# A convolution and expert kernel: the second product token-major, its rows returned by way of HBM, halo and store issues moved between the queues

## The reference

```python
x = x + conv3x3(gn(x), L0_weight) + L0_bias
x = x + conv3x3(gn(x), L1_weight) + L1_bias
h = gelu(einsum('bend,edf->benf', gn(x), w1) + b1)   # exact gelu; e = channel, n = image row, d = 256 columns
x = x + einsum('benf,efd->bend', h, w2) + b2         # f = 1024
x = x + conv3x3(gn(x), L3_weight) + L3_bias
```

## Time and profile before

| | |
|---|---|
| median of 3 runs | 577.23 us |
| the profiled execution's own time | 576.91 us |
| its span, first to last instruction | 575.1 us |
| TensorE busy | 520.0 us, 90% |
| VectorE, ScalarE, GpSimd busy | 374.1, 291.8, 159.1 us |
| steps 0 to 7 with the first transposes | 0 to 143 us |
| first expert, pair 0 | 143 to 178 us |
| experts to the end of the second part | 178 to 447 us |
| third and fourth part | 447 to 499 us |
| steps 8 to 11 and the stores | 499 to 575 us |

### The profile page before, as it was taken

The page is one execution under the profiler, slowest core; times in us unless marked ns, Lnnn a source line. Parts: engine busy times, 40 slices in busy tenths (PEclk is TensorE's granted clock), DMA queues, the critical chain, the costliest instruction groups (busy, mean ns, idle before and its releaser), DMA issues.

```text
span 575.1 us, 9042 instructions
## 1 busy us (share of the span) xinstructions
PE 520.0 (90%) x3326; PEld 255.5 (44%) x3326; DVE 374.1 (65%) x644; ACT 291.8 (51%) x354; POOL 159.1 (28%) x181
## 2 busy tenths in 40 slices
PE   0879999896979999999999999999999989978990
PEld 0534445364544444444444444444444545445440
DVE  4969999888766395194293392481547598678541
ACT  2599988333635453353362361461444828766510
POOL 4679888853270000000000000000000001677610
PEclk9889999898899999999999999999999999989996
DMA  8845555533020122022011112102123300134769
GB/s 327 324 111 146 150 132 139 143 101 147 0 75 1 73 74 74 0 73 73 0 73 73 31 42 73 73 0 73 74 74 108 112 0 2 45 81 107 242 200 349
DMA packets 14168, 57.41 MB, mean 100 GB/s; under 512 B 3116, under 2 KB 3244, under 8 KB 11052
## 3 DMA queue, kind: packets, MB, share of 16 engines
q1 hardware_dynamic: 11820, 49.30, 26.9%
q10 hardware_dynamic: 2316, 7.68, 3.7%
HBM read 30.03 MB, written 8.39 MB: 67 GB/s over the span
## 4 chain that ended last, share of the span: by engine, by line
PE 62%; DVE 19%; ACT 5%; POOL 4%; DMA 3%; issue 2%; ACTq 1%; SPq 1%; POOLq 0%; DVEq 0%
PE PS L1007 28%; PE PS L978 27%; DVE X L665 6%; DVE ST L626 6%; PE PS L878 2%; POOL XN L360 2%; ACT XN L439 2%; PE PS L952 2%; DMA X<-x 2%; PE PS L936 2%; PE PS L885 1%; DVE X L681 1%; ACT SCR L444 1%; DVE XT L674 1%; DVE SM L641 1%
## 5 line engine op out<-in xcount | busy, mean ns | idle before, releaser
L978 PE MATMUL PS<-XT,W1S 128*128 (+1 forms) x768 | 172.0, 383 | 1.7 <-DVE XT L674 1.7
L1007 PE MATMUL PS<-HID,W2S 128*128 128x512 f16 x768 | 170.8, 379 | 1.6 <-DVE W2S L688 1.6
L476 ACT ACTIVATE SCR<-PS,CONST 128x512 f32<-128x512 f32 x128 | 87.0, 686 | 64.4 <-PE PS L978 27.8
L978 PEld LDWEIGHTS PS<-XT,W1S 128*128 128x128 f16 x768 | 75.6, 99 | 91.1 <-issue 4.7
L1007 PEld LDWEIGHTS PS<-HID,W2S 128*128 128x128 f16 x768 | 75.1, 98 | 87.5 <-issue 1.8
L360 POOL TENSOR_TENSOR XN<-SCR,XN 128x1024 f16<-128x1024 f32 (+1 forms) x61 | 100.4, 1670 | 26.5 <-ACT SCR L444 26.5
L688 DVE SCALAR_TENSOR_TENSOR W2S<-W2F,W2S 128x2048 f16<-128x2048 f32 x10 | 22.9, 2291 | 114.6 <-ACT W2S L472 114.6
L333 POOL MEMSET HALO<- 48x520 f16 x12 | 6.3, 526 | 316.8 <-PE PS L978 316.3
L626 DVE BATCH_NORM_STATS2 ST<-X 128x6 f32<-128x512 f32 x128 | 81.5, 681 | 9.4 <-DMA X<-x 8.2
L439 ACT ACTIVATE XN<-X,SC 128x1024 f16<-128x1024 f32 (+1 forms) x61 | 64.1, 1050 | 33.9 <-POOL SC L351 27.6
L665 DVE SCALAR_TENSOR_TENSOR X<-PS,X 128x512 f32<-128x512 f32 x96 | 59.7, 680 | 21.5 <-PE PS L900 21.5
(11 more groups left out here) (47 smaller groups left out, 442.9 us busy)
## 6 DMA issues: line engine op xcount, KB each, us to landing
W1F<-w SPq DMA_DIRECT2D x10, 1024.0 KB, 4.7
W2F<-w SPq DMA_DIRECT2D x10, 1024.0 KB, 4.8
HALO<-XN SPq DMA_DIRECT2D x48, 129.9 KB
out<-X ACTq DMA_DIRECT2D x12, 512.0 KB, 6.8
HALO<-XN SPq DMA_DIRECT2D x48, 121.8 KB
X<-x SPq DMA_DIRECT2D x2, 2048.0 KB, 19.0
HALO<-XN SPq DMA_DIRECT2D x42, 64.9 KB
HALO<-XN SPq DMA_DIRECT2D x42, 60.9 KB
```

The costliest lines, as they stand in the source:

```text
L476: act.activation(SCR[:, ft % 2, 0:CH], bank(ft % G_RING), ACT.Gelu, bias=BT[:, ds(e * FT + ft, 1)], scale=1.0 / (XS * WS)).then_inc(gelu_o ...
L978: mm = pe.matmul(bank(ft % G_RING), W1S[:, w, h * NF + ft * P:h * NF + (ft + 1) * P], rhs, start=(n == 0), stop=(n == 3 * DH - 1))
L1007: mm = pe.matmul(bank(G2_BANK + h), W2S[:, w, ft * NW + h * P:ft * NW + (h + 1) * P], HID[slot][:, part, ft], start=(ft == 0 and part == 0 ...
```

## The change

- **Second product.** `output` now takes 128 tokens of HID as weights and the 256 features of W2S as the moving operand: for each pair 4 blocks k x 8 tiles x 3 products = 96 matmuls of 256 columns, in place of 48 of 512. A block's sum lies in bank 4 + k % 2, and ScalarE copies it out (`copy_out`, [128 tokens, 256]); 64 such copies stand for 32 of [128, 512].
- **The way back.** There are no result transposes. SyncE stores each block to a scratch tensor `yd` in HBM (64 DMAs of 128 KB, in rows of 512 bytes); an image is then read back into YX in four DMAs: the rows of experts 0 to 6 (two of 56 x 16 KB, issued by ScalarE) and the rows of expert 7 (two of 8 x 16 KB, issued by SyncE). VectorE adds YX to X (`add_outputs`, both inputs in SBUF) and takes the statistics. The bias b2 is added to X beforehand, one image in each of experts 1 to 4 (`add_bias`, 32 instructions of VectorE).
- **Halos and stores.** ScalarE now issues the thirds of the first half of every step 8 to 11, between its fourth and fifth piece (4 DMAs a step); SyncE issues the thirds of the second half, step 11's too. All stores are SyncE's: image 0 and the first half of image 1 before the halos of step 11, the rest behind them.
- **Order.** In step 7 VectorE splits W1 before the statistics of the first half; in the first expert W2's split comes earlier, ScalarE writes half of the high parts of HID, and pre-transposes are spread anew. Step 8 to 11 have 7 PSUM banks in turn, not 5.

The diff, cut to its core:

```diff
-G2_BANK, TR_BANK, STAT_BANK = 4, 6, 5
-L3_BANKS = (1, 2, 3, 0, 4)
+G2_BANK, TR_BANK, STAT_BANK, LAST_STAT_BANK = 4, 6, 5, 6
+L3_BANKS = (1, 2, 3, 0, 7, 4, 5)
-THIRDS_BY_ACT = ((0, 0), (11, 0), (11, 1),)
+THIRDS_BY_ACT = ((0, 0), (8, 0), (9, 0), (10, 0), (11, 0))
...
+        def store_tokens(src, b, k, e, signal):
+            rows = yd[b].rearrange("(w c k r) (t j) -> c k (r t) w j", w=W2, c=NC, k=NBLK, j=NJ)
+            dst = rows[e, k]
+            sp.dma_start(dst, src.rearrange("p (w j) -> p w j", w=W2)).then_inc(signal, 16)
...
+        load_w1(LAST + 3)
+        load_w2(LAST + 3)
+        store_outputs(LAST, 1, BLOCKS * (NPAIR * LAST + 2))
+        load_ones(0)
+        store_last(3, 0)
+        store_last(3, 1)
+        sp.wait_ge(last_out[2], 16 * NBLK)
+        load_last_expert(sp, 2)
+        halo_half(8, 0)
+        store_last(3, 2)
+        store_last(3, 3)
+        halo_half(8, 1)
+        sp.wait_ge(last_out[3], 16 * NBLK)
+        load_last_expert(sp, 3)
+        load_ones(SLOT[9])
+        halos(9)
+        load_ones(SLOT[10])
+        halos(10)
+        store(0, 0)
+        store(0, QUAD)
+        store(1, 0)
+        halos(11)
+        store(1, QUAD)
+        store(2, 0)
+        store(2, QUAD)
...
+        def copy_out(to, k, done):
+            act.wait_ge(g2_mm, done)
+            act.activation(to, bank(G2_BANK + k % 2)[:, 0:NW], ACT.Copy,
+                           scale=1.0 / (HS * WS)).then_inc(yt_ok, 1)
...
+                if (k, ft) == (3, 3):
+                    act.wait_ge(x_new, X_NEW_AT["y", 0, NCH - 1])
+                    first_experts(2, 1)
+            if k == 1:
+                first_experts(0, 0)
+                first_experts(1, 0)
+            elif k == 3:
+                first_experts(3, 1)
...
+        for g in range(9, 12):
+            slot_free(g)
+            for k in range(4):
+                normalise_piece(FIRST_PIECE[g] + k)
+            thirds(g, 0)
+            normalise_piece(FIRST_PIECE[g] + 4)
...
-        def mlp_chunk(b, i):
-            m = NCH * b + i
+        def add_outputs(b, i):
+            if i == 0:
+                dve.wait_ge(y_in[b], 16 * 2 * W2)
             xc = x_chunk(b, i)
-            dve.wait_ge(ty_mm, m + 1)
-            dve.tensor_tensor(xc, bank(TR_BANK + m % 2), xc, ALU.add).then_inc(x_new, 1)
+            dve.tensor_tensor(xc, y_chunk(b, i), xc, ALU.add).then_inc(x_new, 1)
...
             for ft in range(FT):
-                if h == 0:
+                if k == 0:
                     pe.wait_ge(hid_ok, ready + (ft + 1))
-                for part, w in ((0, 0), (1, 0), (0, 1)):
-                    mm = pe.matmul(bank(G2_BANK + h),
-                                   W2S[:, w, ft * NW + h * P:ft * NW + (h + 1) * P],
-                                   HID[slot][:, part, ft],
+                for part, w in PRODUCTS:
+                    mm = pe.matmul(to[:, 0:NW], HID[slot][:, part, ft, tokens],
+                                   W2S[:, w, ft * NW:(ft + 1) * NW],
...
-        def in_third_hidden(ft):
-            if ft in (4, 7):
-                result_transposes(0, (4, 7).index(ft))
...
+        def in_fourth_hidden(ft):
+            if ft == 1:
+                group_mean(12)
+            if ft == 3:
+                group_variance(12)
```

More of the change, by code:

```diff
@@ new lines, in store, with store_last @@
+        def store(b, first):
+            for i in range(first, first + QUAD, 2):
+                sp.wait_ge(x_new, X_NEW_AT["c", 8 + b, i + 1])
+                sp.dma_start(out[b][:, i * CH:(i + 2) * CH], x_chunk(b, i, 2)
+                             ).then_inc(out_done, 16)
+        def store_last(n, k):
+            p = ENDING[n][1]
+            b = 2 * p + k // NBLK
+            sp.wait_ge(yt_ok, BLOCKS * (NPAIR * LAST + n) + k + 1)
+            store_tokens(y_last(p, k), b, k % NBLK, NE - 1, last_out[b])
@@ L585, in _, with thirds @@
-        ending_hidden(3)
+        for n in range(3):
+            ending_hidden(n)
+            for k in range(BLOCKS):
+                ending_out(n, k)
+        ending_hidden(3)
+        def thirds(g, half):
+            s = SLOT[g]
+            act.wait_ge(pads_ok[s], 2)
+            act.wait_ge(zero_ok[s], 4)
+            act.wait_ge(conv_mm, 2 * NCH * (HAD[g] + 1))
+            act.wait_ge(lo_ok, PIECE_OF[g, NCH - 1 if half else QUAD] + 1)
+            halo_thirds(act, s, half * NT // 2, (half + 1) * NT // 2, (halo_a, halo_b)[half][s])
@@ L709, in _ @@
             for i in range(0, NCH, QUAD):
-                for m in PREPARED.get((g, i, 0), ()):
-                    xt_low(m)
+                for place in range(2):
+                    for m in PREPARED.get((g, i, place), ()):
+                        xt_low(m)
                 for k in range(QUAD):
@@ L723, in _ @@
                     split_low(W1F, W1S, w1_in, w1_hi, w1_ok, 0)
+                else:
+                    for k in range(0 if g < 7 else -QUAD, QUAD):
+                        conv_stats(g, i + k)
+                if i == 0 and g < 6:
+                    deviation(3 + g)
             aggregate(4 + g)
@@ L760, in _ @@
         next_w1(1)
[L761 removed]
+        dve.wait_ge(pre_ok, NB * NCH)
+        with dve.Fori(1, NB + 1) as e:
             w2_parts(e)
@@ L765, in _ @@
             next_w1(e + 1)
+            add_bias(e)
+        w2_parts(NB + 1)
+        for p in range(NPAIR):
+            hidden(NB + 1, p)
+        next_w1(NB + 2)
         def ending_hidden(k, extra=None):
             e, p, load = ENDING[k]
-            dve.wait_ge(g2_mm, 4 * LAST + 2 * k - 2)
+            dve.wait_ge(g2_mm, BLOCKS * (2 * LAST + k - 1))
             for ft in range(FT):
@@ L1097, in in_fourth_output @@
                 group_mean(13)
-            if h == 1 and ft == 5:
-                group_variance(13)
-        between = ((None, None), (None, None), (in_third_hidden, in_third_output),
-                   (in_fourth_hidden, in_fourth_output))
-        for k, (e, p, _) in enumerate(ENDING):
-            hidden(e, p, between[k][0], k)
-            for h in range(DH):
-                output(e, p, h, between[k][1], k)
-        def results(b, first, last):
-            for i in range(first, last + 1):
-                result_transposes(b, i)
@@ L1112, in last_centres @@
-        def last_centres(g, i, n):
-            if n is not None:
-                group_mean(n)
-            for k in range(QUAD):
-                centre(g, i + k)
-                if n is not None and k == 0:
-                    group_variance(n)
-        results(2, 0, 1)
-        before_step(8)
-        last_centres(8, 0, None)
-        results(2, 2, 5)
-        tiles(8, 0)
-        results(2, 6, 7)
-        last_centres(8, QUAD, 14)
-        results(3, 0, 1)
-        tiles(8, QUAD)
-        results(3, 2, 5)
```

469 lines of the change are left out of this document (243 added, 226 removed).

## The result

The changed kernel takes **605.57 us** (median of 4 runs, 604.84 to 606.65) beside 576.85 for the kernel before: a ratio of 1.050 (95% interval 1.048 to 1.053). The prediction was 583.1 with a range of 572 to 598: the right sign, but the slowdown is 28.7 us and not 6, outside the range. The profiled execution's span is 603.8 us, 28.7 over the earlier trace rows's execution, so the two traces can be compared piece by piece.

A forecast was written before the change was run, and what follows sets the result against it. TensorE was taken to bound the middle, with other engines deciding in the first expert, third part, steps from 8 and drain. Terms −1 (A and B), 0 (front), +8.8 (C), −1.6 (D) gave +6.2 on 576.9: 583.1 us, range 572 to 598.

The forecast's parts named there:

- A: Second product in 256-column matmuls: 109 ns apart, two costing 2.6 ns more than one of 512; +2.0 us.
- The rival of loads that hide behind nothing: Second product: no weight load overlaps a matmul, 205 ns each; 149 us more, some 726 us, chance 0.01.
- B: Experts' middle and end, copies, stores and no result transposes: with A's +2.0 in, step 8 starts at 489.4, −1 us.
- C: Steps 8 to 11: ScalarE's four halo issues ahead of each fifth piece lengthen the steps; +8.8 us in sum.
- Step 8 to 9: Part of C: halo issues add 2.8 us, less 0.8 that GpSimd waits for VectorE's statistics; +2.0.
- the read-back of image 2: Image 2's return through HBM before step 10: adds, statistics and reading leave 7 us for a store to land; 0.
- Step 9 to 10: Part of C: halo issues add 2.8 us, one GpSimd operation beside adds from SBUF costs 2.0; +4.8.
- Step 11: Part of C: this step had ScalarE's halo issues before the change; 0.
- D: Drain behind the last low part: halo issues, stores and end take 20.9 us where 22.5 were; −1.6.
- The front: Step 7 and first expert, new order: can give back at most 7.9 us or lose about 4; taken as 0.
- the third: Rival: image 2's way through HBM is late, step 10 starts 3 to 8 us later; 586 to 592, chance 0.07.
- The first: Rival: first expert gets faster as TensorE waits less and its clock holds; up to 7.9 us gained, chance 0.22.

The follow-up runs named there:

- a1: Changed kernel with SyncE's load of the fourth part's W1 moved ahead of its waits for landing and expert 7's rows; 600.91 us.
- a3: a1, with image 0's first three adds moved behind the W1 split and images 0 and 1 each read back whole by one SyncE load; 594.54 us.
- b4: Kernel before, with ScalarE issuing the four halo DMAs of the first halves of steps 8, 9 and 10; 583.58 us against 575.88.
- b1: Changed kernel with VectorE making the variance of step 9 ahead of its first two adds of image 2; 602.73 us.
- d2: b3 with the second input of images 2 and 3's adds taken from a PSUM bank, not the rows read back; 579.26 us.
- c4: Kernel before, with the adds of images 2 and 3 reading X twice from SBUF, not the transposed result in PSUM; 580.59 us beside 576.89.
- b3: a3 with the edits of b1 and a4, and images 2 and 3 also read back whole by SyncE; 587.48 us.
- a4: Changed kernel with the four halo DMAs of the first halves of steps 8, 9 and 10 issued by SyncE again, not ScalarE; 600.64 us.
- c2: b3 with images 0 and 1 read back in two loads of 64 rows each, not one of 128; 592.82 us.
- d3: b3 with step 8's second updates ahead of all adds of image 3, then its eight adds and eight statistics; 590.04 us.

## Why the prediction was wrong, point by point

**A** was right: two pairs' 192 matmuls of 256 columns with 192 loads take 20.96 us, 109.2 ns each (109 predicted).

```profile
219.03 20.96 PE PS L1138 x192
```

The rival of loads that hide behind nothing is refuted for this form. So is, as it stands, the sentence that the Trainium skill has for it ("TensorE: Matmul & The Clock Gate", Part 3, section "The mechanism": loads overlap matmuls in flight only when the row groups differ); the same section also names a background weight buffer as a second way, which the prediction left out.

**B failed, and with it the forecast:** +12.7 us where −1 stood, 13.7 too little. Two sentences of it are wrong. "The 64 stores are issued by SyncE, which has only the weights' loads there": they were counted, but not the waits for landing and the read-back that stand in the same queue ahead of the fourth part's W1 load. "Without that cover, a wait for W1 would come first" named what then happened, and gave it no price. Mending the waits (a1 to a3) takes away 12.7 of the 13.2 us that were lost between the first expert and step 8. What is left, 313.04 us, is 1.5 over the 311.5 that the −1 amounts to: the rest of B's sum was near.

**C** holds for what it priced: 6.8 us for twelve issues, 7.7 measured in b4. Step 8 to 9 failed: +2.0 predicted, +7.1 measured. The step that failed is "I take 0" for the read-back of image 2. It read the rows at 375 GB/s (5.6 us) and left 7 us for a store. But between 506 and 516 us the DMA engines moved 196 GB/s at a share of 0.86; the store took 8.1 us, and behind it the last 256 KB, expert 7's rows, took 6.8. And it asked when step 10 needs image 2, and not what stands behind the wait for it on VectorE: the variance of step 9. b1 shows that at 5.3 us for this step.

Step 9 to 10 was +4.8 predicted and +6.0 measured. The one collision that was counted (2.0) is there: GpSimd's first operation of the scale took 2.23 us for 0.56, beside adds.

```profile
545.18 2.23 POOL L443 TENSOR_TENSOR RS<-SM,RS 128x1 f32<-128x1 f32 x1
```

```profile
544.51 2.48 DVE L796 TENSOR_TENSOR X<-YX,X 128x512 f32<-128x512 f32 x4
```

Of the rest, 1 us is GpSimd's first four low parts of step 9, which took 7.50 us beside image 2's adds and 6.49 in d2. The other direction, adds that last longer beside GpSimd, was not in the prediction. It cost 3.7 us in c4 and some 8.2 in b3, both directions together, but it is no part of the 28.7: in the changed kernel every four adds of images 2 and 3 took 2.48 us, or 1.29 for two. It came up where a wait or the issues had been taken away, as in b1 (6.23 us) and a4 (8.07). Since the waits overlap, what the single edits take away doesn't add up to 28.7.

**Step 11** was given 0 and took 2.5: ScalarE's four issues lasted 5.26 us, beside and behind SyncE's six stores of 512 KB. The first of these stores was issued 4.4 us ahead of them. In a4, b3 and c2 it was issued 6.9 us ahead: ScalarE's four took 3.3 to 3.4 us, and step 11 15.8 to 16.0. In d3 it was 13.6 us ahead: 2.70 and 15.3. That fits the stores as the cause, though no run moves them alone. In a4, b3 and d3 the drain then took 21.9 us and not 20.5.

```profile
573.47 5.26 ACTq L281 DMA_DIRECT2D HALO<-XN  x4
```

**D** was right: −2.0 where −1.6 stood. One thing in it was not foreseen: ten matmuls of its chain took 0.42 us for 0.21, at a granted clock of 0.53 (about the lower level, 1.2 GHz) between 583.5 and 588 us, after TensorE had waited for a halo. Whether these 2 us cost time is open: in b3 the same matmuls took 0.20, and the drain was no shorter.

**The front** seems to come out at 0 (177.45 for 177.90), but by luck of two executions: over all of them it is some 1.7 us slower, within the prediction's "about 4". Which part of it costs that is not shown.

**Of the rivals** the third (the way through HBM is late, chance 0.07, 586 to 592) had the mechanism, at too small a price and at the wrong step: it looked at step 10, the wait bit in the third part and in step 9. The first, a faster front, did not occur: the granted clock there was 1.00 and not 0.90 (0.93 in b4 and c4), as it said, but the stretch ended hardly earlier (177.5 us for 177.9; b4 and c4, with the old front, 176.1 and 176.3):

```profile
142.30:177.50 35.20, 29.39 (x219) 21.75 (x217) 27.85 (x50) 20.60 (x35) 16.70 (x24) 1.00 0.28 101
```

## What to carry to other kernels

When a queue gets a wait for a landing, list everything that stands behind it in that queue, and on the engine that waits for the data, and give each its due time; both large errors here were a prefetch and a small scalar step that stood behind a wait for something else. Take the rate of a new DMA from a row of the same form, partitions included. An add whose input moves from PSUM to SBUF is as long by itself (0.68 us), but was up to three times as long beside GpSimd's low parts; ask what will run beside it once other waits are gone.

## What was unexpected of the hardware

- Loads into half of the partitions: 214 GB/s at a full DMA share, against 412 for all 128 (c2 and b3). Stores of 128 KB in 512-byte rows landed after 15.9 us beside such loads, after 1.8 where none ran; a load of 1 MB after 12 to 17 us and not 5. (Behind two whole images, in b3, W2's 1 MB took 14.9 us too: what stands ahead counts as well.)
- Four adds of VectorE with two SBUF inputs took 2.50 us alone and 7.72 beside GpSimd's five low parts; with one input in PSUM (d2) 2.46 beside them.
- Four halo issues of ScalarE took 2.8 us in steps 8 to 10 and 5.26 in step 11, behind stores of 3 MB.
- After the first expert the kernel before repeats to 0.01 us up to step 8 in three executions, while the start of the first expert's second pair moves by 1.8: a difference in the front needs more than one execution of each.
